# Sixteen blocks of tokens, routed to expert tiles in two sets: the first set takes eleven blocks, not ten

## The reference, cut to what matters

```
x = x + delta_rule_attention(layernorm(x))       # recurrent over the tokens, 16 heads of 16
x = x + mixture_of_experts(layernorm(x))         # 32 experts, 8 per token, plus a shared expert
x = x + state_space(layernorm(x))                # softplus(x W).mean -> decay; linear scan, 16 states
x = x + quantized_linear(layernorm(x))           # x in blocks of 32 rounded to an fp6 grid, then x W + b
```

```
final[t] = sum over e of  w[t,e] * (silu(x[t] Wg[e]) * (x[t] Wu[e])) Wd[e]
```

## Time and profile before

| | before |
|---|---|
| median of 3 runs | 3337.65 us (3329.45 to 3344.46) |
| the profiled execution's own time | 3336.92 us |
| its span, first to last instruction | 3335.1 us |
| TensorE busy | 2639.5 us, 79% of the span |
| VectorE busy | 2149.0 us, 64% |
| ScalarE busy | 1573.9 us, 47% |
| GpSimd busy (issuing transfers) | 1050.3 us, 31% |
| mean granted TensorE clock | 0.862 of full speed |

### The profile page before, as it was taken

How to read it: one execution, slowest core, us unless ns; L and a number is a source line. 1 busy time by engine, 2 the same in 40 slices (tenths; PEclk the granted TensorE clock), 3 DMA queues, 4 the chain that set the end, 5 groups by cost and what they waited for, 6 DMA issues and landing times.

```text
span 3335.1 us, 109892 instructions
## 1 busy us (share of the span) xinstructions
PE 2639.5 (79%) x46188; PEld 1988.5 (60%) x46188; DVE 2149.0 (64%) x4701; ACT 1573.9 (47%) x2632; POOL 1050.3 (31%) x1028
## 2 busy tenths in 40 slices
PE   4568888887878878787799999998888888845354
PEld 2345555565555556555578888887776666723232
DVE  4879888888998888897332222222466555657675
ACT  5445545455555445552244444444654455523232
POOL 0000333333333333333221121103565544146660
PEclk8778988888888888887799999999999899977676
DMA  7000111111111114111379999999878777623331
GB/s 255 8 10 23 51 62 62 58 63 63 64 56 49 63 60 151 65 55 57 133 260 341 340 345 341 344 323 330 268 254 263 229 250 233 194 87 102 98 96 29
DMA packets 240351, 511.81 MB, mean 153 GB/s; under 512 B 38770, under 2 KB 63860, under 8 KB 239732
## 3 DMA queue, kind: packets, MB, share of 16 engines
q1 hardware_dynamic: 133396, 270.32, 24.5%
q0 software_dynamic: 49152, 134.28, 12.2%
q10 hardware_dynamic: 57312, 100.16, 8.3%
HBM read 303.82 MB, written 200.80 MB: 151 GB/s over the span
## 4 chain that ended last, share of the span: by engine, by line
DMA 53%; PE 22%; DVE 8%; issue 8%; ACT 3%; SPq 3%; POOL 1%; ACTq 0%; DVEq 0%; POOLq 0%
DMA scr_xs<-xn_r,idx 37%; DMA yg<-scr_ys,idx_y 15%; PE ps L637 9%; PE ps L645 4%; PE ps L626 2%; DVE x L1835 2%; POOL yg L922 1%; PE ps L739 1%; DVE tmp L1492 1%; DVE tu L1495 1%; DMA xt<-scr_xs 1%; PE ps L389 1%; DVE conv L1422 1%; SPq L874 1%; PE ps L699 1%
## 5 line engine op out<-in xcount | busy, mean ns | idle before, releaser
L903 POOL DMA_INDIRECT scr_xs<-xn_r,idx x512 | 534.7, 1044 | 1670.4 <-DMA scr_xs<-xn_r,idx 1338.2
L922 POOL DMA_INDIRECT yg<-scr_ys,idx_y x512 | 515.4, 1007 | 537.4 <-DMA yg<-scr_ys,idx_y 266.6
L637 PE MATMUL ps<-xT,wr 128*128 128x256 f32 x2544 | 614.7, 385 | 0.0
L1785 DVE TENSOR_TENSOR h<-sg,ps 128x256 f32<-128x256 f32 x318 | 131.9, 419 | 672.6 <-ACT sg L1156 672.0
L637 PEld LDWEIGHTS ps<-xT,wr 128*128 128x128 f32 x2544 | 470.6, 194 | 62.4 <-issue 8.8
L645 PE MATMUL ps<-wr,h 128*128 128x256 f32 x1272 | 334.0, 386 | 48.5 <-ACT y L967 34.5
L1835 DVE SCALAR_TENSOR_TENSOR x<-yg,wsel,x 128x256 f32<-128x256 f32 x512 | 247.4, 485 | 160.2 <-DMA yg<-scr_ys,idx_y 140.6
L1156 ACT ACTIVATE sg<-ps 128x256 f32<-128x256 f32 x318 | 122.0, 384 | 399.0 <-PE ps L637 398.0
L645 PEld LDWEIGHTS ps<-wr,h 128*128 128x128 f32 x1272 | 242.7, 192 | 89.6 <-issue 41.5
L967 ACT ACTIVATE y<-ps 128x512 f32<-128x512 f32 x318 | 189.8, 597 | 184.7 <-PE ps L645 184.7
L459 PE MATMUL ps<-sq,w_proj 128*128 128x512 f32 x512 | 251.5, 628 | 4.1 <-ACT raw L1008 1.5
(11 more groups left out here) (232 smaller groups left out, 4173.6 us busy)
## 6 DMA issues: line engine op xcount, KB each, us to landing
wr<-in_wexp SPq DMA_DIRECT2D x318, 384.0 KB, 4.7
xt<-scr_xs SPq DMA_DIRECT2D x318, 256.0 KB, 4.4
scr_ys<-y ACTq DMA_DIRECT2D x318, 256.0 KB, 4.6
scr_xs<-zeros SPq DMA_DIRECT2D x128, 256.0 KB, 3.4
x_in<-in_x SPq DMA_DIRECT2D x64, 128.0 KB
x_res<-in_x SPq DMA_DIRECT2D x64, 128.0 KB
scr_xs<-xn_r,idx POOLq DMA_INDIRECT x512, 3.2
scr_x<-x_res SPq DMA_DIRECT2D x16, 512.0 KB
```

The lines of the kernel that those rows point to most:

```text
L637: last = pe.matmul(ps[:, bank, half * TILE:(half + 1) * TILE], wr[:, t % NW, at:at + EI], xT2[:, t % NH, k, :], start=k == 0, stop=k == G - 1)
L903: nc.gpsimd.indirect_dma_start(xs[int(i >= FIRST)][:, :], bass.IndirectOffsetOnAxis(idx[:, i % NR, c, k:k + 1], 0), xn_r[:, i % NR, c, :], ...
L922: nc.gpsimd.indirect_dma_start(yg[:, n % NG, k, :], None, ys[h][:, :], bass.IndirectOffsetOnAxis(idx_y[:, i, c, k:k + 1], 0))\
```

## The change

FIRST goes from 10 to 11, in the two places where it is worked out. The number of tiles stays 318, but set 0 has 207 and set 1 has 111. SL follows: (127 + 2 - 30) // 8 = 12 before, (111 + 2 - 30) // 9 = 9 after. So before, iterations 0 to 7 of the tail loop ran 12 tile slots each and iteration 8 the last 3. After, iterations 0 to 8 run 9 each and iteration 9 the last 2. `tables(0)` and the clearing of set 0's ends come one block later, and block 10's gathers belong to set 0.

```diff
-    if "P" in on and on["P"] + 1 in (NB * 5 // 8, NB):
+    if "P" in on and on["P"] + 1 in (NB * 11 // 16, NB):
         on["H"] = int(on["P"] + 1 == NB)
...
-    FIRST = NB * 5 // 8
+    FIRST = NB * 11 // 16
```

## The result

The changed kernel takes 3296.17 us in the median of 4 runs (3292.97 to 3298.95), the kernel before beside it 3338.68 (3329.45 to 3344.46). The ratio is 0.9859, with a 95% interval of 0.9821 to 0.9897: 1.4% faster. The forecast was 3308 with a range of 3284 to 3334. The profiled execution took 3298.7 us, its span is 3296.9, so 38.2 us less than before, where 29.8 were forecast.

What follows compares the result with a forecast made beforehand. No engine bounds the whole; a chain of stretches does: tile-only TensorE, the tail loop, then the gathers. +48.5 for moved tiles, -24.5 for the loop, -53.8 for one block's gathers make -29.8 us: 3308, range 3284 to 3334.

Steps and rivals of the forecast that it cites:

- the attention stage: Before the first tile: one more block scattered first, no wait expected; counted as nothing, up to 10 us either way.
- The tiles that move: Tile-only stretch: sixteen tiles at 3.03 us delay the first gather and all behind it by 48.5 us.
- One iteration fewer: After the second set is stored: five blocks' gathers left instead of six, -53.8 us.
- Where the tiles end in the iteration: Last tiles due at units 3 and 5: second set stored some 14 us behind the scan, not 22.1.
- The iterations: Tail loop beside the second set: 58 us an iteration with 9 tiles, bounds 54 and 64.6.
- The walk: One tail-loop iteration followed through its engines with the tiles' new places: 54.7 us at the full clock.
- a cold stretch of 3.65 us: Charged once an iteration for TensorE's lower clock behind a wait of some 4.3 us before `skips`.
- TensorE as the bound: Rival for the tail loop: TensorE sets 59.1 us an iteration, -21 us, 3317 in all; chance 0.14.
- nothing back: Rival: tiles taken out of the loop save no time, 64.6 us an iteration, +23 us, 3361; chance 0.05.
- the third rival: Clock falls twice an iteration, before `skips` and round the turn and `deltas`: 62 us, 3340 in all; chance 0.13.
- The full-clock rival: Loop keeps its full clock and meets the gathers at 54 us an iteration: -62 us, 3276; chance 0.14.
- The gathers kept up: Rival denied this: set 0's gathers lose their lead at 58 us; under 10 us effect, no chance of its own.

Runs made afterwards that it cites:

- e2: The changed kernel with 12 tiles an iteration instead of 9: median 3433.94 us, ratio 0.9961 to the kernel before on that chip.
- e3: The changed kernel with 10 tiles an iteration instead of 9: median 3386.24 us, ratio 0.9826 to the kernel before on that chip.
- e5: The changed kernel with 10 tiles an iteration, run again on another chip: median 3411.99 us, ratio 0.9854 to the kernel before there.
- e7: The changed kernel with three gathers in flight for all blocks: median 3623.62 us, ratio 1.0423 to the kernel before on that chip.
- c2: The changed kernel unchanged, as control on a further chip: median 3579.70 us, beside 3455.94 for the kernel before there.
- e8: The changed kernel with two gathers in flight in every block: median 3455.78 us, ratio 1.0048 to the kernel before on that chip.

## Why the prediction was right, point by point

The changes against the profiled span of before, forecast and measured:

| step | forecast, us | measured, us |
|---|---|---|
| sixteen tiles in the tile-only stretch, and the attention stage | +48.5 | +53.4 |
| first gather to scan 0 | 0 | +1.6 (106.4 for 104.8) |
| scan 0 to the second set stored | -24.5 | -38.6 (517.8 for 556.4) |
| one block's gathers | -53.8 | -52.8 (270.0 for 322.8) |
| last gather to the end | 0 | -1.8 (75.9 for 77.7) |
| sum | -29.8 | -38.2 (span: -38.2) |

The miss of 8.4 us is less than that of its largest part: the loop gave 14.1 us more than forecast, and the delay ahead of it took 4.9 us more, which hid some of it.

- **The tiles that move: right.** The excess of 4.9 us is not theirs. 6.7 us of it were there before any tile ran, in the attention stage, which I had counted at nothing, up to 10 us either way. No run here separates what in that stage is late. The tiles themselves gave 46.7.
- **One iteration fewer: right.** Five blocks at 54.0 us. That the gathers pace this stretch was shown from outside too: where POOL was ahead, e2's and e3's iterations without tiles took 39.1 to 39.5 us, and 49 to 54 once the lead was gone (50.4 and 51.5 in between).
- **Where the tiles end in the iteration: right.** POOL's wait ended 13.9 us behind scan 9; 14 was forecast.
- **The iterations: right in mechanism, mis-sized in one term.** The walk gave 54.7 us and a cold stretch of 3.65 us, taken from line 730 in the earlier trace rows, rounded to 58. Measured are 56.3. The wait of 4 us before `skips`, the clock at its lower level behind it, the vanished wait at line 730 and the places of the later steps came as walked: in block 4's iteration the second `quant_rows` at 16.1 us after `skips` began (13.2 plus the cold stretch of 2.7), `deltas` at 27.9 (25.3), the scan at 56.9 (54.7). The walk's 19.35 us for the roots, for which no row is shown, holds too: the turn of `xa` began at 25.7, so 22.9 without the cold stretch, for 22.7. What failed is "I charge one such stretch as before, 3.65 us": behind `skips` it costs 1.64 or 2.74 us, and the loop takes part of that back. Eight iterations at 1.7 us less are 13.3 us, more than the whole miss of 8.4.
- **Why the 3.65 us were too much.** The prediction reads them as one fall at line 730, in an iteration that else runs "at the full clock". The windows of before, in the iterations of blocks 4 and 7, show more:

```profile
2657.70:2664.50 6.80, 6.80 (x13) 4.33 (x14) 2.29 (x9) 0.00 (x0) 3.46 (x4) 0.50 0.46 163
2664.50:2674.70 10.20, 8.19 (x42) 6.92 (x41) 4.75 (x17) 8.21 (x15) 6.18 (x8) 1.00 0.79 248
2674.70:2678.20 3.50, 3.17 (x15) 2.68 (x13) 2.06 (x4) 3.28 (x8) 1.75 (x2) 0.51 0.81 246
2847.90:2876.10 28.20, 23.99 (x141) 18.73 (x142) 16.12 (x45) 11.58 (x22) 12.30 (x13) 1.00 0.73 232
2876.10:2879.50 3.40, 3.40 (x14) 2.89 (x14) 1.99 (x5) 3.32 (x9) 0.00 (x0) 0.50 0.74 225
```

  Block 4's iteration has a second stretch at the lower clock, round the turn, and block 7's 64.6 us hold one too, so they are no full-clock iteration. The 3.65 us are the price of 6.9 us more at the lower level (10.3 against 3.4), about half of it. Nor is line 730's own time the sign of it: in block 2's iteration it took 1.12 us behind its second wait, at the full clock, and the clock fell only behind it; that iteration took 68.6 us, with 10.2 us at the lower level in three stretches. In the changed kernel the stretch round the turn is gone in all eight iterations, and the one behind `skips` is there in all of them, 6.8 us long in every second one and 3.4 in the others. That is the alternation of 57.0 and 55.7 us.
- **e5 shows the same term from the other side.** With a tenth tile the iteration of block 7 took 55.0 us, all of it at the full clock. PE's timeline at its start, with the wait down to 2.05 us, then the windows over the iteration:

```profile
3000.90 1.16 PE L750 MATMUL ps<-d_diag,xT 128*128 128x128 f32 x8 [2.05 <-DVE d_bx L1858]
3002.32 1.16 PE L750 MATMUL ps<-d_diag,xT 128*128 128x128 f32 x8 [0.26 <-ACT quantT L967]
3003.41 1.93 PE L759 MATMUL ps<-w_cs,hs 32*32 32x256 f32 x32
```

```profile
3000.90:3055.80 54.90, 49.32 (x296) 38.51 (x296) 40.51 (x84) 33.58 (x59) 33.43 (x33) 1.00 0.74 238
```

  A tile more, and the iteration is 1 us shorter than the 56.3 of nine tiles. It ran on another chip, with POOL far ahead, so the 1 us is not shown to be the clock's alone; e3's three iterations of ten tiles without a fall took 54.2 to 55.4. The Trainium skill, page "TensorE: Matmul & The Clock Gate", section "HAM oscillation — how this bites in real kernels", has the loop falling cold in every round behind its idle gap. The changed kernel's rows agree, 0.50 behind each wait of 3.9 us. The price here is 1.6 to 2.7 us a round.
- **The rivals.** TensorE as the bound (59.1) and "nothing back" (64.6) are excluded by 56.3. The second cold stretch round the turn, which the third rival expects from the change, was there before it and went with it; `deltas` took 3.67 us, as before at the full clock. The full-clock rival (54) did not come with nine tiles; e5 comes near it with ten. The gathers kept up, but not by much: POOL waited 0.6 us for DVE in all nine iterations, so the ring was never full, and DVE waited 0.2 us for a gather. Between the issue of the last gather of a block's fourth chunk and its first sum lay 4 to 6 us for blocks 2 to 4 and 18 to 20 for blocks 8 to 10, against 2.8 to 2.9 where POOL has no lead. In before it was over 50 us from block 5 on.
- **What no term of the prediction held** is the chip. On two others the same change costs 3% or more in the medians of four (3563 beside 3449, 3580 beside 3456); the lowest of the four (3480, 3471) are above the medians of the kernel before too, but by 0.9% and 0.4% only. That the forecast met a chip on which it holds is luck. The long iterations go with bursts of gathers and late results of TensorE, and two in flight ended them; that the shorter iterations are what brings them on is argued, not shown. Why those chips do so and the first in none of its four executions stays open. e7's stall shows TensorE itself starting its products late, beside gathers and without tiles. In c2's iteration the records have its products at their usual pace and only the marks late, and there it is not shown which is true: the ends of products are modelled in the records, and the traces of those chips also lack many landing marks of gathers (3943 of 8192 in c2, 8156 in the changed kernel on the first chip; 6569 with two in flight, e8), so that both kinds of mark suffer together. Whether the recording itself, or the fetching of TensorE's instructions, has a part in it was not looked at. Nor was a kernel tried that keeps three in flight and spaces them out, which is what the cycle above suggests. No trace of the kernel before exists on those chips, so its own 76 to 118 us more there are not broken down. The attention stage has part of it: the first tile's load came at 1671 to 1704 us in the twelve later traces, at 1641.7 in the first.

Of all versions, eleven blocks with a pace of 10 and three gathers in flight is the one that was faster than the kernel before on both chips where it ran: 1.7% and 1.5% by the ratios, 0.8% and 1.1% by the medians, with intervals that end close to no change. It was not run on the first chip.

## What to carry to other kernels

When work is taken out of a loop that waits in a chain through several engines, walk the chain with the new places of the work; the engine's busy share would have given 59.1 us here and the walk gave 54.7, with 56.3 measured. Price a fall to the lower clock by the instructions that will stand behind the new wait, and look at the clock over the whole iteration before calling one cold stretch the difference. And a split that is tuned to a few microseconds of slack should be measured on more than one chip: this one is 1.4% faster on one and, by the medians, over 3% slower on two.

## What the runs showed of the hardware

- With three indirect gathers in flight beside expert tiles, three chips showed results of TensorE that reached ACT up to 40.1 us (e3) after the recorded end of the products, and iterations of 77 to 117 us in place of 54 to 57. With two in flight, on one of the three, that was gone but for one tile in each run.
- With three in flight and no tiles, TensorE once started only 26 products in 66.8 us, at a clock of 0.50, with nothing shown that it waited for (e7).
- A gather of 128 rows costs POOL 1.7 us with two in flight and no tiles, 1.3 with three (84.0 us for 64, e7), and 2.1 with two in flight beside tiles on the last chip (e8).
- A wait of 3.9 us was followed by the clock at 0.50 in all eight iterations of the changed kernel that have one, and one of 2.05 us was not, in the iteration of e5 shown. Behind a wait of 2.2 to 2.4 us line 730 ran at the lower clock in four of the seven iterations of blocks 1 to 7 of before.
- The same two products, `skips` and `outputs`, took 6.58 and 5.48 us behind such a wait and 3.84 at the full clock.
